# First-stage norms moved from DVE to ACT, and a new order of work at the stage's edges

## The chip, the cores and the metric

One core of a Trainium2 chip runs one program of 38,066 instructions. The engines are PE (TensorE), DVE (VectorE), ACT (ScalarE), POOL (GpSimd) and SP (SyncE, which here only issues DMAs); each takes its own instructions in order, and they meet at semaphores. The metric is the device time of one execution in microseconds (us).

## The reference, cut to what matters

16 batches of 112 tokens of width 256 pass through four blocks, each added to its input:

```python
x = x + tanh(g_xattn[0]) * L0_xattn(layernorm(x), ctx_1024, mask, ...)   # 16 heads of 16, 375 keys
x = x + tanh(g_ffn[0])   * L0_ffn(layernorm(x), Wg, We, be)              # 8 experts, the best 2 weighed
x = x + tanh(g_xattn[1]) * L1_xattn(ctx_1024, layernorm(x), ...)         # 16 heads of 64
x = x + tanh(g_ffn[1])   * L1_ffn(layernorm(x), W1, b1, W2, b2, Wr, br)  # routed experts
# layernorm(x) = (x - mean) / sqrt(var + 1e-5)
```

The first two lines are the kernel's first stage; the change lies in it. Both of its layer norms are of a [112, 256] tile, one row per token.

## The kernel before

The program has three stages, one after the other: `phase_attention_small_heads` (tiles named a_, the first 455 us), `phase_attention_large_heads` (b_) and `phase_experts` (c_). The first loops over 16 batches. Each engine has its own `body(b, par)`, and on PE, ACT and DVE a body has 16 slots, one per head. The order within an engine is written out by hand; there is no scheduler. In slot s of batch b:

- PE: scores of head s (L610), transposes of the probabilities of head s-2 (L618), values of head s-4 (L632), then items;
- DVE: `maxima` of head s (L853), `plo` of head s-2 (L858), the low half of the transposed probabilities;
- ACT: `exps` of head s-1 (L717), `phi` of head s-2 (L724), the high half of the same.

Numbers are carried as two f16 halves, high and low. `plo` of a head needs `phi` of that head, `phi` needs PE's transposes, and these need the exponential. The scores have two buffers, so PE can be at most two heads ahead of DVE.

In between, the slots hold the projections of the next batch (`item`, P_K keys, P_XT the transposed tokens, P_Q queries, P_V values: table PSLOT) and the expert block of the batch before (`ditem`: D_XT, D_GATE, D_PAIRS, D_CWT, D_BIAS: tables DSLOT and DREAD). On ACT the items of a slot stand ahead of its exponential.

The two norms. For the tokens of batch b+1: DVE's `stats_x` and `moments_x` in slot 0 (L813, L817), POOL's `deviation_x` (L431 variance plus eps, L433 the power -1/2), DVE's `norm_x` at the end of slot 1 (L823), then PE's transposes (L549). For x1, the output of the attention of batch b-1: POOL's `residual` makes x1 (L456, L459, L463), DVE's `stats_x1` in slot 5 (L874, L876), POOL's `deviation_x1` (the same lines), DVE's `norm_x1` at the end of slot 6 (L829), PE's transposes (L580), ACT's and DVE's halves (L701, L882), the gate and the four products of pairs of experts (L527, 128x512).

The weights of the second stage are read from HBM in eight loads of 512 KB (`load_next`, ACT's queue, L740, in the even batches from 2 on and once more in batch 14) and split in 16 parts: `next_high` on ACT (L746) in slots 8 to 15 of batch 14 and 0 to 7 of batch 15, `next_low` on POOL (L473) inside `sum_experts`. The buffer `next_f` first holds the expert weights of this stage (`we_f`, 2 MB), read at the start by ACT's queue and split in batch 0 (L734, L468).

Keys and queries pass through HBM to be stacked: SP writes them out (`keys_out` L342, `queries_out` L356) and reads them back in six DMAs each (`stack_keys` L350, `stack_queries` L364). SP's order for batch 0 is: load the tokens and context of batch 1 (L325, L327), keys out, key stacks, queries out, query stacks. ACT, before its items of batch 0, waits for the setup loads and takes the tanh of the gates (L793); DVE does `norm_x(0)` between the low halves of the weights, copies bq, waits for the tanh, and then does its items.

Of the kernel before, what the change touches and what calls it, by code (L numbers as in the profile page):

```python
# [64 lines left out]
def need(eng, sem, per, batch, count, met=None):  # L65

    need_all(eng, met, (sem, per, batch, count))
# [29 lines left out]
def ahead(b, n):  # L99

    return not (isinstance(b, int) and b + n > B - 1)

def phase_attention_small_heads(nc, x, ctxT, mask, g_xattn, g_ffn, wq, wk, wv, bq, bk, bv, wg, we, be, consts,
# [3 lines left out]
    with ExitStack() as ctx:  # L107
# [40 lines left out]
        rstd = sb("rstd", [T, 1], F32)  # L148
        xn = sb("xn", [T, D], F32)
# [32 lines left out]
        rstd1 = sb("rstd1", [T, 1], F32)  # L182
        xn1 = sb("xn1", [T, D], F32)
# [103 lines left out]
                 14: [D_PAIRS[3]], 15: [D_BIAS]}  # L287

# [14 lines left out]
        def _(sp):  # L303
# [93 lines left out]

            load_tokens(1)
            keys_out(0, 0)
            stack_keys(0, 0)  # L400
            queries_out(0, 0)
# [10 lines left out]
        def _(pool):  # L412
# [15 lines left out]
            def deviation(c, s_in, s_mid, s_out, stat, mid, out):  # L428

                need(pool, s_in, 2, c, 2, settled)  # L430
                pool.tensor_scalar(mid[:, :], stat[:, 1:2], 1.0, EPS, ALU.mult, ALU.add).then_inc(s_mid, 1)  # L431
                need(pool, s_mid, 1, c, 1)
                pool.tensor_tensor(out[:, :], mid[:, :], neg_half[0:T, :], ALU.pow).then_inc(s_out, 1)  # L433

            def deviation_x(c):
                deviation(c, s_stats, s_var, s_rstd, mv, var, rstd)

            def deviation_x1(c):
                deviation(c, s_stats1, s_var1, s_rstd1, mv1, var1, rstd1)
# [35 lines left out]
            def sum_experts(c, alone=True):  # L475

                for j in range(E // 2):
                    if not alone:
                        for n in range(2):
                            next_low((c - (B - 3)) * 8 + 2 * j + n)  # L480
                    need(pool, s_scaled, E // 2, c, j + 1)
                    need(pool, s_odd if j else s_x2, E // 2 if j else 1, c, j)
                    pool.tensor_tensor(acc_odd[:, :], scaled[j % 2][:, :], (acc_odd if j else x1)[:, :], ALU.add).then_inc(s_odd, 1)
                need(pool, s_odd, E // 2, c, E // 2)
                need(pool, s_dfree, DI, c, DI)
                need(pool, s_store, 16, c, 0)
                pool.tensor_tensor(x2[:, :], acc_odd[:, :], acc[:, :], ALU.add).then_inc(s_x2, 1)

            def body(b, par):
                if ahead(b, 1):  # L490
                    deviation_x(b + 1)
                if not first(b):
                    residual(b - 1)
                    deviation_x1(b - 1)
                if ahead(b, 1):
                    mask_bias(b + 1, 1 - par)
                    split_queries(b + 1)
                if ahead(b, 2):
                    split_context(b + 2)
                if not first(b):  # L500
                    sum_experts(b - 1, ahead(b, 2))
                if first(b):
                    for n in range(H // 2):
                        experts_low(n)
# [168 lines left out]
        def _(act):  # L673
# [40 lines left out]

            def exps(b, par, h):
                need(act, s_max, H, b, h + 1)
                act.activation(prob[:, h % RING, :], prob[:, h % RING, :], ACT.Exp, bias=top[:, h % RING:h % RING + 1],  # L717
                               scale=-1.0, accum_out=sums[par][:, h:h + 1]).then_inc(s_exp, 1)
# [17 lines left out]
            def load_next(col):  # L736


                act.wait_ge(s_welo, H // 2)
                act.dma_start(next_f[:, bass.ds(col, NLOAD)], next_w_dram[:, bass.ds(col, NLOAD)]).then_inc(s_nload, 16)  # L740

            def next_high(n):

                if n == 0:
                    act.wait_ge(s_nload, 16 * 8)
                act.activation(next_w[:, HI, n * NEXT:(n + 1) * NEXT], next_f[:, n * NEXT:(n + 1) * NEXT], ACT.Copy).then_inc(s_nhi, 1)  # L746
# [6 lines left out]
            def body(b, par):  # L753
                for s in range(H):
# [14 lines left out]
                    if par == 0 and not first(b) and s == 0:  # L769
                        load_next(b * (NLOAD // 2) - NLOAD)  # L770
                    if isinstance(b, int) and b == B - 2 and s == H // 4:
                        load_next(b * (NLOAD // 2))
                    if not ahead(b, 2) and (s >= H // 2) == ahead(b, 1):
                        next_high((s + H // 2) % H)
# [13 lines left out]
            for n, (lo, hi) in enumerate(WPARTS):  # L788
                act.wait_ge((s_wk, s_wq, s_wv)[n], 32 if n else 16)
                act.activation(wqkv[:, HI, :, lo:hi], wqkv_f[:, :, lo:hi], ACT.Copy).then_inc(s_whi, 1)  # L790
            act.wait_ge(s_const, 50)
            act.wait_ge(s_setup, NSETUP)
            act.activation(tanhs[:, :], gates[:, :], ACT.Tanh).then_inc(s_tanh, 1)  # L793
            act.dma_start(we_f[:, :, :], we).then_inc(s_wload, 16)
            for k in range(PI):
                item(0, 0, k)
# [4 lines left out]
            out_lo(B - 1)  # L801
            ditem(B - 1, D_XT)
# [5 lines left out]
        def _(dve):  # L808
# [9 lines left out]

            def norm_x(c):

                need(dve, s_rstd, 1, c, 1)
                need(dve, s_item, PI, c, 0)
                dve.tensor_scalar(xn[:, :], x_in[:, :], mv[:, 0:1], rstd[:, 0:1], ALU.subtract, ALU.mult).then_inc(s_xn, 1)  # L823

            def norm_x1(c):

                need(dve, s_rstd1, 1, c, 1)
                need(dve, s_ditem, DI, c, 0)
                dve.tensor_scalar(xn1[:, :], x1[:, :], mv1[:, 0:1], rstd1[:, 0:1], ALU.subtract, ALU.mult).then_inc(s_xn1, 1)  # L829
# [101 lines left out]
            def body(b, par):  # L931
                for s in range(H):
# [21 lines left out]
                    if ahead(b, 1) and s == 1:  # L954
                        norm_x(b + 1)
                    if not first(b):
                        if s == 9:
                            rank_experts(b - 1)
                        if s == 5:
                            stats_x1(b - 1)  # L960
                        if s == 6:
                            norm_x1(b - 1)

# [3 lines left out]
            for n, (lo, hi) in enumerate(WPARTS):  # L967
                dve.wait_ge(s_whi, n + 1)
                dve.tensor_tensor(wqkv[:, LO, :, lo:hi], wqkv_f[:, :, lo:hi], wqkv[:, HI, :, lo:hi], ALU.subtract).then_inc(s_wlo, 1)
                if n == 0:  # L970
                    stats_x(0)
                    moments_x(0)
                if n == 1:
                    norm_x(0)
            dve.wait_ge(s_const, 48)
            for e in range(2):
                rows = slice(64 * e, 64 * e + 64)
                dve.tensor_copy(bq_c[rows, :], bq_g[rows, e::2]).then_inc(s_const, 1)
# [3 lines left out]
            for k in range(PI):  # L982
                item(0, 0, k)
# [5 lines left out]
            norm_x1(B - 1)  # L989
# [1365 lines left out]
```

## Time and profile before

| | |
|---|---|
| median of 3 runs | 1407.45 us (1403.61 to 1407.69) |
| profiled execution | 1406.79 us, its span 1405.0 us |
| PE busy | 1225.0 us (87%) |
| DVE busy | 1083.2 us (77%) |
| ACT busy | 999.4 us (71%) |
| POOL busy | 813.3 us (58%) |

The span is what the trace covers; the profiled execution's time lies 1.8 us above it. Busy shares are means over three stages with different limits. In a timeline row the first number is the start in us, the second the duration; an instruction can start some 0.1 us before the one ahead of it on its engine ends. Ends of matmuls are modelled.

### The profile page before, as it was taken

Reading aid. Unit: us, or ns where it says so; the run is one execution under the profiler, and the core shown is the slowest. Engines: PE = TensorE matmul, PEld = TensorE weight load, DVE = VectorE, ACT = ScalarE, POOL = GpSimd, SP = SyncE. Lnnn points to the kernel's source line nnn. Section 1 sums busy time; section 2 is a strip of 40 time slices with the busy share of each in tenths; the row PEclk is TensorE's granted clock in tenths of the full one; section 3 lists DMA queues with packets and bytes.
Section 4 is the critical chain, followed back from the end, with each engine's and each line's share of the span. In section 5 each row is a group of like instructions: output and inputs, shape, how many; then the busy total and the mean of one; then the engine's idle time right before and its main releaser. Section 6 shows DMA issues by size and latency. Waiting matters only on the chain. (4 is left out here: it accounts for less than half of the span.)

```text
span 1405.0 us, 38066 instructions
## 1 busy us (share of the span) xinstructions
PE 1225.0 (87%) x13060; PEld 880.3 (63%) x13060; DVE 1083.2 (77%) x3112; ACT 999.4 (71%) x2552; POOL 813.3 (58%) x1204
## 2 busy tenths in 40 slices
PE   3999999999986499999999999999999974489994
PEld 1777777777764245566656566656666653389894
DVE  3799999999985168888888888888888882477872
ACT  2888888888883358877787887787888771256562
POOL 3544444444454346677777777777777674146564
PEclk7799999999987599999999999999999985699997
DMA  5444545455420148877788777878777793854333
GB/s 162 131 146 144 148 120 169 114 151 155 134 50 7 49 94 156 141 147 146 153 158 160 143 146 154 147 151 163 152 144 152 137 196 61 316 154 60 57 36 76
DMA packets 309406, 185.50 MB, mean 132 GB/s; under 512 B 257930, under 2 KB 295186, under 8 KB 306112
## 3 DMA queue, kind: packets, MB, share of 16 engines
q1 hardware_dynamic: 293024, 140.82, 47.3%
q0 software_dynamic: 13168, 35.80, 10.5%
q10 hardware_dynamic: 3024, 6.47, 1.5%
q8 instruction: 106, 1.74, 0.5%
q14 instruction: 84, 0.69, 0.2%
HBM read 76.19 MB, written 49.94 MB: 90 GB/s over the span
## 5 line engine op out<-in xcount | busy, mean ns | idle before, releaser
L1682 ACT ACTIVATE b_prob<-b_prob,b_top 112x487 f32<-112x487 f32 x256 | 178.9, 699 | 28.3 <-DVE b_top L1808 26.5
L1315 POOL TENSOR_TENSOR b_halves<-b_prob,b_halves 112x487 f16<-112x487 f32 x128 | 146.9, 1148 | 83.7 <-ACT b_halves L1707 82.2
L1493 PE MATMUL b_ps_p<-w_s,b_tok_s 128*128 128x512 f16 (+1 forms) x768 | 187.7, 381 | 4.0 <-DVE b_k_s L1795 3.2
L1493 PE MATMUL b_ps_p<-b_tok_s,w_s 128*128 128x487 f16 x768 | 181.9, 374 | 6.6 <-POOL b_tok_s L1309 3.7
L1808 DVE CUSTOM_DVE_ANT_0 b_prob<-b_ps_s,b_keep 112x487 f32<-112x487 f32 x256 | 167.3, 655 | 13.2 <-PE b_ps_s L1586 11.6
L717 ACT ACTIVATE a_prob<-a_prob,a_top 112x375 f32<-112x375 f32 x256 | 154.8, 605 | 3.7 <-DVE a_top L853 2.0
L1707 ACT ACTIVATE b_halves<-b_prob 112x487 f16<-112x487 f32 x256 | 156.0, 609 | 0.6
L853 DVE CUSTOM_DVE_ANT_0 a_prob<-a_ps_s,a_keep 112x375 f32<-112x375 f32 x256 | 138.1, 540 | 21.7 <-PE a_ps_s L610 21.4
L618 PE MATMUL a_ps_t<-a_const,a_prob 112*125 112x112 f32 x768 | 135.7, 287 | 10.6 <-ACT a_prob L717 9.1
L1601 PEld LDWEIGHTS b_ps_o<-b_v_s,b_pT 128*128 128x128 f16 (+1 forms) x3072 | 123.9, 99 | 31.4 <-DMA b_pT<-b_halves 11.6
L1601 PE MATMUL b_ps_o<-b_v_s,b_pT 128*128 128x64 f16 (+1 forms) x3072 | 135.0, 195 | 9.2 <-DMA b_pT<-b_halves 9.1
L858 DVE TENSOR_TENSOR a_pT<-a_ps_t,a_pT 125x336 f16<-125x336 f32 x256 | 128.1, 500 | 19.2 <-ACT a_pT L724 18.7
L618 PEld LDWEIGHTS a_ps_t<-a_const,a_prob 112*125 112x125 f32 x768 | 117.5, 196 | 36.1 <-ACT a_prob L717 28.1
L1493 PEld LDWEIGHTS b_ps_p<-b_tok_s,w_s 128*128 128x128 f16 x768 | 66.0, 98 | 95.1 <-issue 20.3
L1493 PEld LDWEIGHTS b_ps_p<-w_s,b_tok_s 128*128 128x128 f16 (+1 forms) x768 | 70.7, 105 | 83.5 <-DVE b_k_s L1795 12.5
L1795 DVE TENSOR_TENSOR b_k_s<-b_ps_p,b_k_s 128x487 f16<-128x487 f32 x128 | 84.5, 661 | 49.9 <-ACT b_k_s L1663 49.9
L1813 DVE TENSOR_TENSOR b_halves<-b_prob,b_halves 112x487 f16<-112x487 f32 x128 | 120.9, 945 | 0.0
L724 ACT ACTIVATE a_pT<-a_ps_t 125x336 f16<-125x336 f32 x256 | 113.5, 443 | 2.3 <-PE a_ps_t L618 2.2
L1670 ACT ACTIVATE b_v_s<-b_ps_p 128x512 f16<-128x512 f32 (+1 forms) x128 | 76.2, 595 | 53.1 <-PE b_ps_p L1493 52.1
L1803 DVE TENSOR_TENSOR b_v_s<-b_ps_p,b_v_s 128x512 f16<-128x512 f32 (+1 forms) x128 | 87.9, 686 | 31.7 <-ACT b_v_s L1670 31.7
L1586 PE MATMUL b_ps_s<-b_k_s,b_q_s 64*112 64x487 f16 x768 | 107.1, 385 | 0.3 <-DVE b_top L1808 0.3
L1663 ACT ACTIVATE b_k_s<-b_ps_p 128x487 f16<-128x487 f32 x128 | 72.8, 570 | 41.6 <-PE b_ps_p L1493 40.2
(263 smaller groups left out, 3022.9 us busy)
## 6 DMA issues: line engine op xcount, KB each, us to landing
xs<-a_blank SPq DMA_DIRECT2D x14, 1032.0 KB, 4.5
c_w_pool<-w_split SPq DMA_DIRECT2D x8, 1600.0 KB, 10.6
b_wch_f<-in_w_experts POOLq DMA_DIRECT2D x32, 384.0 KB, 5.2
w_split<-b_wch_s POOLq DMA_DIRECT2D x32, 384.0 KB, 3.9
a_k_stack<-keys SPq DMA_DIRECT2D x96, 93.8 KB, 3.1
a_ctx_f<-in_ctxT SPq DMA_DIRECT2D x16, 375.0 KB, 3.8
keys<-a_k_s SPq DMA_DIRECT2D x16, 375.0 KB, 3.2
b_ctx_t<-in_ctx SPq DMA_DIRECT2D x16, 375.0 KB
```

Source lines behind the costliest of these rows:

```text
L618: last = pe.transpose(ps_t[h % 2][0:KB0, j * T:(j + 1) * T], prob[:, h % RING, j * KB0:(j + 1) * KB0], ident[0:T, 0:T])
L717: act.activation(prob[:, h % RING, :], prob[:, h % RING, :], ACT.Exp, bias=top[:, h % RING:h % RING + 1], scale=-1.0, accum_out=sums[par][ ...
L724: act.activation(pT[0:KB0, h % RING, HI, :, 0:T], ps_t[h % 2][0:KB0, 0:NB0 * T].rearrange("p (j n) -> p j n", j=NB0), ACT.Copy).then_inc(s ...
L853: dve.tensor_tensor_reduce(prob[:, h % RING, :], ps_s[h % 2][0:T, 0:C], keep[par][:, :], -SCALE0, 3e38, ALU.add, ALU.min, top[:, h % RING: ...
L858: dve.tensor_tensor(pT[0:KB0, h % RING, LO, :, 0:T], ps_t[h % 2][0:KB0, 0:NB0 * T].rearrange("p (j n) -> p j n", j=NB0), pT[0:KB0, h % RIN ...
L1315: pool.tensor_tensor(halves[:, h % TURN, LO, 0:NK], prob[:, h % RING, 0:NK], halves[:, h % TURN, HI, 0:NK], ALU.subtract).then_inc(s_lo[1], 1)
L1493: last = pe.matmul(out, sta(a, k), mov(m, k), start=(k == 0 and n == 0), stop=(k == tiles - 1 and n == 2))
L1601: last = pe.matmul(ps_o[h // 8][:, col:col + D1], pT[0:k, h % TURN, a, j, :], v_s[par][0:k, m, j, h * D1:(h + 1) * D1], start=(h % 8 == 0 ...
L1682: act.activation(prob[:, h % RING, 0:NK], prob[:, h % RING, 0:NK], ACT.Exp, bias=top[:, h % RING:h % RING + 1], scale=-1.0, accum_out=sums ...
L1707: act.activation(halves[:, h % TURN, HI, 0:NK], prob[:, h % RING, 0:NK], ACT.Copy).then_inc(s_hi, 1)
L1808: dve.tensor_tensor_reduce(prob[:, h % RING, 0:NK], ps_s[h % 3][0:T, 0:NK], keep[par][:, :], -SCALE1, 3e38, ALU.add, ALU.min, top[:, h % R ...
L1813: dve.tensor_tensor(halves[:, h % TURN, LO, 0:NK], prob[:, h % RING, 0:NK], halves[:, h % TURN, HI, 0:NK], ALU.subtract).then_inc(s_lo[0], 1)
```

## The change

It adds two 112x1 tiles for each norm, `away` (minus the mean) and `shift` (minus the mean times the reciprocal deviation). POOL computes both, one operation ahead of the power and one behind it. ACT computes `rstd * x + shift` in place of DVE's `(x - mean) * rstd`: for the tokens in slot 1, for x1 in slot 6, each time ahead of the slot's exponential. The weights of the second stage are loaded one part per batch in batches 2 to 9 and split two parts per batch in batches 4 to 11, on ACT in slots 2 and 6, on POOL after `split_queries` and after `sum_experts`. At the start SP sends keys and queries out first and only then issues the stacks; ACT and DVE do the items of batch 0 ahead of the tanh and of what waits for the setup loads; the 2 MB load of the expert weights is issued in slot 1 of batch 0.

```diff
@@ sync @@
+            keys_out(0, 0)
             load_tokens(1)
-            keys_out(0, 0)
+            queries_out(0, 0)
             stack_keys(0, 0)
-            queries_out(0, 0)
             sp.wait_ge(s_zq, 2)
             stack_queries(0, 0)
@@ gpsimd @@
-            def deviation(c, s_in, s_mid, s_out, stat, mid, out):
+            def deviation(c, s_in, s_mid, s_out, stat, mid, out, off, shift):
                 need(pool, s_in, 2, c, 2, settled)
                 pool.tensor_scalar(mid[:, :], stat[:, 1:2], 1.0, EPS, ALU.mult, ALU.add).then_inc(s_mid, 1)
-                need(pool, s_mid, 1, c, 1)
+                pool.tensor_scalar(off[:, :], stat[:, 0:1], -1.0, None, ALU.mult).then_inc(s_mid, 1)
+                need(pool, s_mid, 2, c, 2)
                 pool.tensor_tensor(out[:, :], mid[:, :], neg_half[0:T, :], ALU.pow).then_inc(s_out, 1)
+                need(pool, s_out, 2, c, 1)
+                pool.tensor_tensor(shift[:, :], off[:, :], out[:, :], ALU.mult).then_inc(s_out, 1)
...
                     split_queries(b + 1)
+                if 0 <= b - NEXT_SPLIT < H // 2:
+                    next_low(2 * (b - NEXT_SPLIT))
                 if ahead(b, 2):
                     split_context(b + 2)
                 if not first(b):
-                    sum_experts(b - 1, ahead(b, 2))
+                    sum_experts(b - 1)
+                if 0 <= b - NEXT_SPLIT < H // 2:
+                    next_low(2 * (b - NEXT_SPLIT) + 1)
@@ scalar @@
+            def norm_x(c):
+                need(act, s_rstd, 2, c, 2)
+                need(act, s_item, PI, c, 0)
+                act.activation(xn[:, :], x_in[:, :], ACT.Identity, bias=shift[:, 0:1], scale=rstd[:, 0:1]).then_inc(s_xn, 1)
...
-                    if par == 0 and not first(b) and s == 0:
-                        load_next(b * (NLOAD // 2) - NLOAD)
-                    if isinstance(b, int) and b == B - 2 and s == H // 4:
-                        load_next(b * (NLOAD // 2))
-                    if not ahead(b, 2) and (s >= H // 2) == ahead(b, 1):
-                        next_high((s + H // 2) % H)
+                    if first(b) and s == 1:
+                        act.dma_start(we_f[:, :, :], we).then_inc(s_wload, 16)
+                    if s == 0 and 0 <= b - NEXT_LOAD < H // 2:
+                        load_next(b - NEXT_LOAD)
+                    if s in NEXT_SLOTS and 0 <= b - NEXT_SPLIT < H // 2:
+                        next_high(2 * (b - NEXT_SPLIT) + NEXT_SLOTS.index(s))
+                    if ahead(b, 1) and s == 1:
+                        norm_x(b + 1)
+                    if not first(b) and s == 6:
+                        norm_x1(b - 1)
                     if not (first(b) and s < 1):
                         exps(*heads(s, 1, b, par))
...
+            norm_x(0)
             act.wait_ge(s_const, 50)
+            for k in range(PI):
+                item(0, 0, k)
             act.wait_ge(s_setup, NSETUP)
             act.activation(tanhs[:, :], gates[:, :], ACT.Tanh).then_inc(s_tanh, 1)
-            act.dma_start(we_f[:, :, :], we).then_inc(s_wload, 16)
-            for k in range(PI):
-                item(0, 0, k)
@@ vector @@
-                    if ahead(b, 1) and s == 1:
-                        norm_x(b + 1)
-                        if s == 6:
-                            norm_x1(b - 1)
```

DVE's copies of bq move ahead, behind the first moments, and its items of batch 0 ahead of the tanh, in the same way as ACT's. `norm_x1` on ACT has the form of `norm_x`. NEXT_LOAD is 2, NEXT_SPLIT 4, NEXT_SLOTS (2, 6).

## Rows read from the trace of the kernel before

**Rows 1.** Busy time of each engine in stretches: us, then busy us (instructions), granted clock, DMA.

```profile
257.31:260.72 3.41, 2.81 (x30) 2.19 (x28) 3.41 (x11) 3.32 (x11) 1.47 (x3) 1.00 0.42 117
180.00:240.00 60.00, 55.79 (x594) 45.42 (x595) 56.94 (x200) 51.83 (x158) 25.75 (x41) 1.00 0.51 148
```

**Rows 2.** Timeline of DVE, L813 in batch 2 and in batch 14: start, duration, instruction.

```profile
83.50 0.42 DVE L813 BATCH_NORM_STATS2 a_bns<-a_x_in 112x6 f32<-112x256 f32 x1
...
379.98 0.42 DVE L813 BATCH_NORM_STATS2 a_bns<-a_x_in 112x6 f32<-112x256 f32 x1
```

**Rows 3.** Timelines of ACT, POOL and DVE, slots 0 to 1 of one batch.

```profile
257.17 0.60 ACT L717 ACTIVATE a_prob<-a_prob,a_top 112x375 f32<-112x375 f32 x1
257.76 0.44 ACT L724 ACTIVATE a_pT<-a_ps_t 125x336 f16<-125x336 f32 x1
...
257.45 0.19 POOL L431 TENSOR_SCALAR a_var<-a_mv 112x1 f32<-112x1 f32 x1 [0.94 <-DVE a_mv L817]
257.72 0.56 POOL L433 TENSOR_TENSOR a_rstd<-a_var,a_neg_half 112x1 f32<-112x1 f32 x1
...
257.19 0.17 DVE L817 BATCH_NORM_AGGREGATE a_mv<-a_bns 112x2 f32<-112x6 f32 x1
...
258.24 0.50 DVE L858 TENSOR_TENSOR a_pT<-a_ps_t,a_pT 125x336 f16<-125x336 f32 x1
258.65 0.41 DVE L823 TENSOR_SCALAR a_xn<-a_x_in,a_mv,a_rstd 112x256 f32<-112x256 f32 x1
```

**Rows 4.** The same three timelines, slot 6 of that batch.

```profile
264.22 0.60 ACT L717 ACTIVATE a_prob<-a_prob,a_top 112x375 f32<-112x375 f32 x1
...
265.23 0.55 POOL L433 TENSOR_TENSOR a_rstd<-a_var,a_neg_half 112x1 f32<-112x1 f32 x1
...
265.61 0.50 DVE L858 TENSOR_TENSOR a_pT<-a_ps_t,a_pT 125x336 f16<-125x336 f32 x1
266.03 0.50 DVE L829 TENSOR_SCALAR a_xn<-a_x,a_mv,a_rstd 112x256 f32<-112x256 f32 x1
```

**Rows 5.** Groups of instructions by line, 100 to 340 us.

```profile
L712 ACT ACTIVATE a_scaled<-a_ps_p,a_cw 112x256 f32<-112x256 f32 x40 | 19.0, 475 | 13.8 <-PE a_ps_p L527 13.8
```

**Rows 6.** Timeline of all engines, the start of the kernel.

```profile
11.41 0.33 ACTq L794 DMA_DIRECT2D a_next_f<-in_we  x1
...
13.61 0.35 SPq L342 DMA_DIRECT2D keys<-a_k_s  x1
...
20.67 2.68 SPq L350 DMA_DIRECT2D a_k_stack<-keys  x6
...
26.81 2.65 SPq L364 DMA_DIRECT2D a_q_stack<-queries  x6
...
30.82 0.56 PE L610 MATMUL a_ps_s<-a_k_stack,a_q_stack 96*112 96x375 f16 x1 [14.13 <-DMA a_q_stack<-queries]
...
36.96 0.34 SPq L342 DMA_DIRECT2D keys<-a_k_s  x1
...
40.37 3.75 SPq L350 DMA_DIRECT2D a_k_stack<-keys  x6
```

**Rows 7.** Timeline of ACT, POOL and DVE in batch 15.

```profile
415.89 0.67 ACT L746 ACTIVATE w_s<-a_next_f 128x512 f16<-128x512 f32 x1
...
416.56 2.26 POOL L473 TENSOR_TENSOR w_s<-a_next_f,w_s 128x512 f16<-128x512 f32 x2
416.63 2.35 DVE L829 TENSOR_SCALAR a_xn<-a_x,a_mv,a_rstd 112x256 f32<-112x256 f32 x1
```

**Rows 8.** Stretches around a fall of the clock, and expert products at either clock.

```profile
405.11:408.53 3.42, 2.12 (x22) 1.64 (x23) 2.37 (x9) 3.42 (x12) 3.34 (x4) 1.00 0.00 0
408.53:411.94 3.41, 3.26 (x24) 2.46 (x23) 2.42 (x8) 3.41 (x11) 0.73 (x2) 0.50 0.24 67
...
269.14 1.48 PE L527 MATMUL a_ps_p<-a_we_s,a_x1T 128*112 128x512 f16 x6
...
422.33 2.79 PE L527 MATMUL a_ps_p<-a_we_s,a_x1T 128*112 128x512 f16 x6
```

## What I predict, and why

> **What bounds the kernel now.** The change touches only the first stage, about the first third of the page's slices, so I read that stage and nothing else: first the starts of one repeated DVE instruction, then the timelines of DVE, ACT, POOL and PE over one batch, then the start, the end and the granted clock. The statistics of the next batch's tokens are taken once per batch, just after a batch begins. From batch 2 to batch 14 there are 13 of them, and first and last lie 296.48 us apart, 24.71 us per batch [rows 2]. Every batch repeats to a hundredth, so what happens in one happens in all. Inside a batch the busy shares differ by part. In the stretch of slots 1 to 3, DVE is busy 3.41 of 3.41 us, ACT 3.32, PE 2.81; over 60 us of whole batches ACT is busy 51.83 [rows 1], so it idles 3.4 us per batch. DVE is full there, and ACT almost: that idle time lies nearly all in slots 9 to 14, beside the expert products. The reader should not take ACT's mean of 71% over the span as room in slots 1 to 8.
>
> The four engines run in lock step. In slot s, PE does scores of head s, DVE its maximum, ACT the exponential of head s-1 and the high half of the probabilities of s-2, DVE their low half. In slot 1 ACT's high half ran from 257.76 to 258.20 and DVE's low half began at 258.24 [rows 3]: 0.04 us of slack. Whatever delays ACT there delays DVE.
>
> **Part 1: the tokens' normalisation moves to ACT, at the head of slot 1.** It removes from DVE one instruction of 0.41 us, of which 0.32 lies on the path (it began at 258.65, and the next instruction starts some 0.1 before one ends) [rows 3]. On ACT it stands behind the first key item and ahead of the exponential of head 0, which began at 257.17 [rows 3]. ACT takes its instructions in order, so both that exponential and the high half behind it wait until the shift is there. When is that? The moments end at 257.36; POOL begins the variance at 257.45 and the power at 257.72, done at 258.28 [rows 3]. The change puts the negated mean between them (one more of 0.19, as the variance takes) and the product after the power: I take 0.25 and 0.30 with the gaps, so the shift lands at about 258.8. ACT can start at 258.85, and a 112x256 activation with a scale column takes 0.475 [rows 5], some 0.35 before the next can follow. So the exponential begins at 259.2 instead of 257.17: +2.03. DVE's low half, bound to ACT by 0.04 us, moves as much; less 0.32 saved, DVE's path is 1.71 us later. Can that be given back in slots 2 to 5? DVE and ACT are both full there, so no. Bounds: +1.2 if the two POOL operations cost only 0.1 each and ACT's own time partly hides, +2.3 if they cost 0.5 each.
>
> **Part 2: the second normalisation moves to ACT in slot 6.** In the same way: ACT reached the exponential of head 5 at 264.22; the power ended only at 265.78; DVE took the product at 266.03, its low half of head 4 having begun at 265.61 [rows 4]. With the shift 0.5 later, ACT normalises at 266.35 and the exponential starts at 266.7, 2.5 us late. ACT then does 0.6 for it and 0.44 for the high half, so the low half begins at about 267.75 instead of 265.61: +2.15. DVE's saving is 0.42, and POOL's mask operation no longer meets it. By adding up the slots I get +1.84 for this part (ACT is a little behind DVE already). Bounds +1.2 and +2.4. Both parts: +3.55 us per batch, in batches 1 to 14: 14 x 3.55 = +49.7. Batch 0 has the first wait only, beside a slower PE: +0.5.
>
> **Part 3: what the two holes do to the clock.** PE waits for the same exponentials: it will be idle about 1.4 us in slot 2 and 2.1 us in slot 7, on top of the small gaps it has. The trace of before has this once. At the batches' end, in slots 0 to 3 of batch 15, PE was busy 2.12 of 3.42 us, after which the clock stood at 0.50, that is 1.2 in place of 2.4 GHz, from 408.5 until dense expert products had run [rows 8]. Around the second hole PE will be less busy than that, so I expect the clock to fall in many batches and to rise again in the expert products. The price is in rows at either level: one such product took 1.48 us at full and 2.79 at half clock [rows 8], 1.3 more. If two of a batch's four run at half and slots 7 and 8 lose 0.5, that is +3.1 per batch, 14 x 3.1 = +43.4. Bounds: 0 (the clock stays) and 4 x 1.3 + 1.1 = 6.3 per batch, +88. I take the middle, since both ends have a row behind them and neither is nearer.
>
> **Part 4: the weights of the next stage.** Before, ACT rounded them 16 times in batches 14 and 15 (0.67 each, some 0.5 without the overlap) and POOL took the rest (2.26 for two) [rows 7]. Now two of each fall into batches 4 to 11. The one in slot 6 lies inside ACT's new wait and is free. The one in slot 2 stands where ACT is full: 8 x 0.5 = +4. POOL's second, at the end of a batch, may hold up the variance by 0.2 of a us, but where the clock is low the first is partly hidden. I take +4; bounds 0 and +6.5. The loads (512 KB each, one per batch) are waited for a batch or more later: nothing, unless the queues fill.
>
> **Part 5: the start.** Before, SP issued keys out at 13.61, and the stacking of keys only at 20.67, 7.1 us later, while ACT's load of 2 MB (issued 11.41) moved. Queries went out after all of the key stacking; their stacking began at 26.81 and the first scores at 30.82 [rows 6]. For the next keys, without that load, it is 36.96 to 40.37, 3.4 us [rows 6]. Now: the shift is ready at 10.5, ACT's key items follow at 10.9 without the wait for gates and tanh, keys go out at 12.8, the key stacks at 16.2; the queries go out at 15.7 in between, their stacks follow the key stacks at 19.1 and land by 23.1. First scores at 23.1 instead of 30.8: -7.7. If the key write takes 7 us also without the big load, little is left: -1. The big load is now issued in batch 0, slot 1, ten us before its first reader and with the key stacks of batch 1 beside it: +0.5, bounds 0 and +4. With batch 0's wait the start is -6.7.
>
> **Part 6: the end of the stage.** In batch 15 the eight roundings made ACT the bound of slots 0 to 7. The DVE product at 416.63 took 2.35 us while POOL's two ran 2.26 [rows 7]: it waited for POOL, and PE with it. Both go, some -4.5 if all counted. But the wait of part 2 comes here as well (+2) and PE at half clock needs about as long as ACT did. The tail has POOL's two extra operations bare, +0.5. I take -1.5, bounds -5 and +2.
>
> For that stall, the Trainium skill ("SBUF — State Buffer", section "Who interferes with whom") says that DVE in some modes and GpSimd share a port pair, and whoever starts first holds it for the whole instruction. The row agrees in kind; but DVE waited for both POOL instructions and not for one, 2.35 us where one would be 1.13. By the page the cure would be worth 1.1 us here, by the row 2.3. It also says that ACT never waits for it, which speaks for the change in batch 15 and nowhere else.
>
> **The sum.** The profiled execution took 1406.8 (span 1405.0), beside a median of 1407.5. 1406.8 - 6.7 + 49.7 + 43.4 + 4 - 1.5 = 1495.7, so 1496.
>
> **The rivals.** A: the waits come, the clock stays up. For it: 13 batches ran at full clock with small gaps. Against: the fall of [rows 8] with a busier PE. 1495.7 - 43.4 = 1452. B: the clock is at half for most of each batch and PE binds throughout, 10 us per batch instead of 3.1: about 1590. Against: expert products raised the clock before. C, on the other side: the normalisations cost nothing on ACT, because it comes to them later than I think, and DVE, which is full [rows 1], gains 0.32 + 0.42 per batch: 1406.8 - 14 x 0.74 - 6.7 - 1.5 = 1388. It decides if ACT reaches the normalisation 1.7 us later against the moments than it does now. Speaks for it: ACT idles 3.4 us per batch. Against: where that lies, and DVE's moments come after the high half that ACT gives it, so ACT is always ahead. D: the change doesn't bring its start (the key write is slow by itself): +6.7 on any of these; it is in the range.
>
> **Chances.** The forecast 0.60 (its own range 1465 to 1540), A 0.25 (1440 to 1465), B 0.08, C 0.07. The range 1440 to 1540 holds the first two. Faster by over 0.3% (about what a measurement can tell from no change) 0.06, within 0.3% 0.02, slower 0.92.
>
> **What would show it.** Parts 1 and 2: on ACT, two idle gaps per batch ended by POOL's shift, 1.6 and 2 us, ahead of the two normalisations; the DVE low half behind them waits for ACT as long; the batch 28 us apart at full clock, 31 to 32 with half-clock stretches. Part 3: the granted clock's mean over 100 to 380 us, 1.00 before, well below it. Part 5: first scores near 23 us. The prediction is wrong if DVE shows no such idle time, or if the batch is 24 us.

## Result and profile after

The changed kernel takes 1470.2 us (median of 4, 1468.6 to 1471.0) beside 1405.5 us (median of 4, 1403.1 to 1407.7): ratio 1.0457, 95% interval 1.0436 to 1.0478, 64.7 us slower. The profiled execution took 1471.0, its span 1469.2 (1405.0 before, 64.2 less than now). I had forecast 1496, with a range of 1440 to 1540. Three runs that took far longer than the others of their kernel (5930.5 and 3288.0 us of before, 1631.9 us in one experiment) stand in no median here.

All of it is in the first stage. Its last addition on POOL (the output of the last batch) began at 454.27 before and begins at 519.06 now, 64.8 later. First the stretch from 60 to 380 us: us, then busy us (instructions) of PE, PEld, DVE, ACT and POOL, granted clock, DMA share, GB/s. Of after:

```profile
60.00:380.00 320.00, 272.44 (x2539) 221.22 (x2537) 245.63 (x860) 239.81 (x714) 144.35 (x239) 0.89 0.42 121
```

and of before:

```profile
60.00:380.00 320.00, 298.89 (x3108) 241.46 (x3106) 302.59 (x1074) 271.61 (x828) 142.37 (x218) 1.00 0.49 141
```

DVE, which was nearly full (302.6 of 320), is now idle for 74 us, and the clock's mean is 0.89. What DVE and the others wait for, 110 to 385 us, after (us in total, times, longest):

```profile
DVE a_pT L874 <- ACT a_pT L747: 53.2, 53, 2.4
...
PE a_ps_t L629 <- ACT a_prob L740: 36.6, 27, 2.3
ACT a_xn L730 <- POOL a_shift L443: 16.5, 9, 1.9
...
ACT a_xn L736 <- POOL a_shift L443: 8.5, 9, 2.1
```

This is the chain of parts 1 and 2: POOL's shift, ACT, DVE and PE. The batches, by the same instruction as [rows 2], in batches 2 and 14 of after:

```profile
80.21 0.42 DVE L841 BATCH_NORM_STATS2 a_bns<-a_x_in 112x6 f32<-112x256 f32 x1
...
443.22 0.42 DVE L841 BATCH_NORM_STATS2 a_bns<-a_x_in 112x6 f32<-112x256 f32 x1
```

That is 363.0 us for 12 batches, 30.25 each, beside 24.71: +66.5. Batch 1 has +2.8, the time up to the statistics of batch 0 -6.1, batch 0 nothing, and from the last statistics to the stage's end it is 75.84 beside 74.29: +1.6. These five make the 64.8.

Slots 0 to 2 of batch 7, timelines of POOL, ACT, DVE and PE (to be held against [rows 3]):

```profile
232.53 1.16 POOL L483 TENSOR_TENSOR w_s<-a_next_f,w_s 128x512 f16<-128x512 f32 x1
233.78 0.19 POOL L438 TENSOR_SCALAR a_var<-a_mv 112x1 f32<-112x1 f32 x1
234.04 0.24 POOL L439 TENSOR_SCALAR a_away<-a_mv 112x1 f32<-112x1 f32 x1
234.37 0.56 POOL L441 TENSOR_TENSOR a_rstd<-a_var,a_neg_half 112x1 f32<-112x1 f32 x1
235.00 0.19 POOL L443 TENSOR_TENSOR a_shift<-a_away,a_rstd 112x1 f32<-112x1 f32 x1
...
235.23 0.60 ACT L730 ACTIVATE a_xn<-a_x_in,a_shift,a_rstd 112x256 f32<-112x256 f32 x1 [1.89 <-POOL a_shift L443]
235.73 0.59 ACT L740 ACTIVATE a_prob<-a_prob,a_top 112x375 f32<-112x375 f32 x1
...
236.78 0.51 DVE L874 TENSOR_TENSOR a_pT<-a_ps_t,a_pT 125x336 f16<-125x336 f32 x1 [2.39 <-ACT a_pT L747]
...
236.47 0.58 PE L629 MATMUL a_ps_t<-a_const,a_prob 112*125 112x112 f32 x3 [1.99 <-ACT a_prob L740]
```

ACT idles 1.89 us for the shift, and behind it DVE idles 2.39 and PE 1.99. POOL's half of a rounded weight (232.53) stands ahead of the variance and holds it until 233.78; the moments were there at 233.43. The second hole, in slot 6 ([rows 4] before):

```profile
244.54 0.62 ACT L769 ACTIVATE w_s<-a_next_f 128x512 f16<-128x512 f32 x1
245.66 0.60 ACT L736 ACTIVATE a_xn<-a_x,a_shift,a_rstd 112x256 f32<-112x256 f32 x1 [0.49 <-POOL a_shift L443]
...
247.22 0.51 DVE L874 TENSOR_TENSOR a_pT<-a_ps_t,a_pT 125x336 f16<-125x336 f32 x1 [1.74 <-ACT a_pT L747]
```

The clock in the same batch, in stretches of 2.2 us ([rows 8] before):

```profile
234.71:236.91 2.20, 0.44 (x4) 0.44 (x5) 0.13 (x1) 1.68 (x5) 1.13 (x3) 1.00 0.34 117
236.91:239.11 2.20, 1.42 (x14) 1.12 (x12) 1.78 (x5) 2.20 (x7) 0.00 (x0) 0.75 0.00 0
239.11:241.31 2.20, 2.20 (x23) 2.09 (x21) 2.20 (x10) 2.20 (x8) 0.00 (x0) 0.50 0.96 256
...
243.51:245.71 2.20, 2.20 (x20) 2.20 (x19) 1.48 (x6) 0.97 (x4) 1.17 (x5) 0.70 0.45 114
245.71:247.91 2.20, 1.35 (x16) 1.05 (x15) 0.69 (x2) 2.20 (x7) 2.05 (x4) 1.00 0.32 72
```

PE stands still for the first hole, its clock falls to 1.2 GHz behind it, it works through slots 3 to 6 at that clock, and is back at 2.4 GHz before the second hole. Around that one (the last row) PE was busy 1.35 of 2.20 us, and the clock stayed; ahead of the fall in [rows 8] it had been busy 2.12 of 3.42. Whole batches: batch 3, and batch 7.

```profile
111.26:142.68 31.42, 27.27 (x242) 22.17 (x241) 23.20 (x82) 22.20 (x66) 11.99 (x22) 0.84 0.40 121
...
232.51:262.54 30.03, 25.85 (x242) 21.24 (x241) 23.23 (x84) 22.90 (x68) 14.20 (x24) 0.89 0.41 125
```

The start ([rows 6] before), all engines:

```profile
11.60 1.01 ACT L701 ACTIVATE a_k_s<-a_ps_p,a_bk_c 128x375 f16<-128x375 f32 x2
...
13.40 0.34 SPq L349 DMA_DIRECT2D keys<-a_k_s  x1
...
17.19 2.79 SPq L357 DMA_DIRECT2D a_k_stack<-keys  x6
...
20.07 2.71 SPq L371 DMA_DIRECT2D a_q_stack<-queries  x6
...
24.71 0.56 PE L621 MATMUL a_ps_s<-a_k_stack,a_q_stack 96*112 96x375 f16 x1 [5.82 <-DMA a_q_stack<-queries]
```

From keys out to the key stacks it is 3.8 us where it was 7.1.

### The profile page after: what moved, and what is told of

Same layout as the page of the kernel before. It is cut to its first block and busy times, and to the rows that moved or that the text cites. A ratio compares the mean times of both kernels' runs of the same rounds, so it can differ in the third digit from the quotient of the medians.

```text
span 1469.2 us, 38137 instructions
## 1 busy us (share of the span) xinstructions
PE 1258.4 (86%) x13060; PEld 908.5 (62%) x13060; DVE 1071.0 (73%) x3080; ACT 1014.5 (69%) x2584; POOL 828.3 (56%) x1268
## 5 line engine op out<-in xcount | busy, mean ns | idle before, releaser
L629 PE MATMUL a_ps_t<-a_const,a_prob 112*125 112x112 f32 x768 | 150.0, 309 | 65.4 <-ACT a_prob L740 63.4
L1690 ACT ACTIVATE b_prob<-b_prob,b_top 112x487 f32<-112x487 f32 x256 | 178.8, 698 | 27.3 <-DVE b_top L1816 25.7
L629 PEld LDWEIGHTS a_ps_t<-a_const,a_prob 112*125 112x125 f32 x768 | 128.2, 214 | 100.7 <-ACT a_prob L740 93.5
L1609 PEld LDWEIGHTS b_ps_o<-b_v_s,b_pT 128*128 128x128 f16 (+1 forms) x3072 | 124.0, 99 | 31.2 <-DMA b_pT<-b_halves 11.9
L538 PE MATMUL a_ps_p<-a_we_s,a_x1T 128*112 128x512 f16 x384 | 102.6, 408 | 1.0
```

Source lines behind the costliest of these rows:

```text
L629: last = pe.transpose(ps_t[h % 2][0:KB0, j * T:(j + 1) * T], prob[:, h % RING, j * KB0:(j + 1) * KB0], ident[0:T, 0:T])
L1609: last = pe.matmul(ps_o[h // 8][:, col:col + D1], pT[0:k, h % TURN, a, j, :], v_s[par][0:k, m, j, h * D1:(h + 1) * D1], start=(h % 8 == 0 ...
L1690: act.activation(prob[:, h % RING, 0:NK], prob[:, h % RING, 0:NK], ACT.Exp, bias=top[:, h % RING:h % RING + 1], scale=-1.0, accum_out=sums ...
```

## Experiments

Three questions: are the waits at the two normalisations the cause, what does the clock add, and what do the rest of the change's parts bring? "Before" was run beside each group; its medians were 1405.5 (the start alone, both back on DVE, six idle products, normalisations later), 1405.4 (each alone, two more POOL operations), 1403.2 (ten idle products and the two with roundings in slots 11 and 14) and 1405.6 (the last). A batch is counted from one statistics instruction to the next, as above.

**The start alone.** Before with only the new order of part 5:

```diff
+            keys_out(0, 0)
             load_tokens(1)
-            keys_out(0, 0)
+            queries_out(0, 0)
             stack_keys(0, 0)
-            queries_out(0, 0)
...
+                    if first(b) and s == 1:
+                        act.dma_start(we_f[:, :, :], we).then_inc(s_wload, 16)
```

and ACT's and DVE's items of batch 0 ahead of the tanh.

> The kernel before with the new order at the start alone (keys and queries out first, items ahead of the tanh, the 2 MB load in batch 0); the norms on DVE, loads and splits of the next weights as before. The first scores moved from 30.8 to 24.7 us, so -6 us if nothing gives it back: 1399 to 1401 us. If the 2 MB load in batch 0 delays the expert weights and batch 1 (rival), less than 3 us is left: 1403 or above.

1399.2 us, ratio 0.9950 (0.9925 to 0.9975). The first scores come at 23.29, every batch from 2 to 13 takes 24.71, and the stage ends 7.9 us earlier than before:

```profile
12.89 0.34 SPq L342 DMA_DIRECT2D keys<-a_k_s  x1
...
19.03 2.72 SPq L364 DMA_DIRECT2D a_q_stack<-queries  x6
...
23.29 0.56 PE L610 MATMUL a_ps_s<-a_k_stack,a_q_stack 96*112 96x375 f16 x1 [7.33 <-DMA a_q_stack<-queries]
```

In after they come at 24.71. Of these 1.4 us, 1.1 comes from the normalisation of batch 0 on ACT, ahead of the key items: with it on DVE and the rest of the change in place (the next kernel) they come at 23.57. The other 0.3 was not followed.

**Both normalisations back on DVE.** After, with `norm_x` and `norm_x1` on DVE as before and POOL's negated mean and product gone; the start and the spread roundings stay.

> The changed kernel with both norms back on DVE and POOL's two added operations gone; start, loads and splits of the next stage's weights as changed. Theory 1 and 2 both expect a batch of 24.7 to 25.2 us and 1395 to 1403 us: everything lost lies in the norms, the start's 6 us is kept. If instead the spread splits cost (theory 3: ACT full in slot 2 of batches 4 to 11), 8 of the batches are 0.5 us longer or more and the time is 1404 or above.

1397.9 us, ratio 0.9939 (0.9916 to 0.9962): 72 us below after. So the two normalisations, with POOL's operations for them, are the whole loss. Batches without roundings are back at 24.71; those with them take 25.38, or 26.3 and 26.4 in two where the clock fell.

**Each alone.** After with only the tokens' normalisation on ACT, and with only that of x1:

> The changed kernel with only the tokens' norm (slot 1) on ACT, x1's back on DVE. Theory 1 prices the wait of slot 1 at 2.0 to 2.5 us per batch less 0.32, and the clock falls behind the hole as before: a batch of 27 to 28.5 us, 1430 to 1450 us. If the wait of slot 1 were absorbed, 1400.

> The changed kernel with only x1's norm (slot 6) on ACT, the tokens' back on DVE. Alone, this wait is not shortened by a slow PE ahead of it, so theory 1 prices it at about 2 us per batch less 0.42 and a part of a clock fall: a batch of 26.3 to 28 us, 1420 to 1445 us. If e5 and e6 together lose more than the changed kernel does, the two waits overlap through the clock; if less, they add to something of their own.

1440.3 (1.0242, 1.0225 to 1.0259) and 1447.3 us (three runs, 1441.5 to 1449.0; 1.0283, 1.0251 to 1.0315), the second somewhat above what I expected. Over 1397.9 they cost 42.4 and 49.3, together 91.7, where both at once cost 72.3. Two delays of one path would add up; these overlap. At full clock they do add: with only x1's on ACT, batch 2 (no roundings, clock 1.00) takes 26.85, 2.14 over 24.71, and this wait is worth 2.11 below, where both are there. What overlaps is the clock's part. With only x1's on ACT the batches come in two kinds, here batches 7 and 8:

```profile
220.29:251.10 30.81, 27.44 (x242) 21.99 (x241) 23.59 (x85) 22.73 (x67) 13.82 (x22) 0.83 0.41 123
251.10:278.34 27.24, 23.38 (x242) 18.64 (x241) 23.30 (x85) 22.34 (x67) 13.80 (x22) 1.00 0.46 138
```

The same instructions take 27.24 us when the clock stays and 30.81 when it falls: 3.6 us for one fall. It fell here behind the hole of slot 7, and stayed at half through slots 8 to 10 and the first expert products:

```profile
235.69:237.89 2.20, 2.20 (x24) 1.95 (x21) 1.75 (x7) 1.51 (x5) 1.34 (x1) 0.50 0.57 158
237.89:240.09 2.20, 2.20 (x7) 1.15 (x6) 1.05 (x6) 0.83 (x4) 0.00 (x0) 0.50 0.08 18
```

PE is busy without a pause, DVE for 1.75 and 1.05 us of the 2.20 and ACT for 1.51 and 0.83: PE sets the pace. That is the term of part 3 much as I had priced it (3.1).

**Two more POOL operations.** After, with two more dependent 112x1 products in each chain, whose result nobody reads:

```diff
...
+                for i in range(2):
+                    need(pool, s_mid, 4, c, 2 + i)
+                    pool.tensor_scalar(spare[:, :], stat[:, 0:1], -1.0, None, ALU.mult).then_inc(s_mid, 1)
...
```

> The changed kernel with two more dependent 112x1 operations on POOL ahead of each power, some 0.55 us more until each shift. If both norms' waits lie bare on the path (theory 1), each batch is 0.8 to 1.1 us longer, 11 to 16 us in all: 1481 to 1487 us. If it is ACT's own work or the clock that sets the batch (theory 2), 0 to 4 us.

1487.1 us, ratio 1.0574 (1.0557 to 1.0592). From the negated mean to the power it is 0.90 us here and 0.33 in after, 0.57 more. Where the clock goes as it does in after, twice 0.57 comes out: batches 5, 7 and 10 take 31.2 us beside 30.0, 1.2 more, so POOL's chain lies bare on the path. The whole, 16.9, is some 30 times 0.57 with 32 normalisations in the stage, but that it fits so well is luck. Batches 2, 3 and 13 are 0.7 to 0.9 shorter than in after, since there no fall came behind the second hole, and batches 6 and 9 are 3.4 and 3.2 longer (33.43 and 33.19), since there one did.

**Idle products in the holes.** After, with PE given six, then ten, products of 512 columns in slots 2 and 7 of batches 1 to 14, ahead of the transposes that wait; their results are never read.

```diff
+                        if s in FILL and ahead(b, 1) and not first(b):
+                            need(pe, s_max, H, b, s)
+                            for i in range(FILL[s]):
+                                pe.matmul(ps_s[(s + 1) % 2][:, 0:512], wqkv[:, HI, 0, 0:128], wqkv[:, HI, 1, 0:512], start=True, stop=True)
```

> The changed kernel with six idle 512-column matmuls on PE (1.3 us at full clock) in each of the two holes of batches 1 to 14, into a score bank that is free there; their results are read by nobody. If the half clock behind the holes costs 1 to 3 us a batch, the clock now stays up more and the time falls by 10 to 30 us, to 1440 to 1460. If the clock's falls cost nothing (the waits alone fill the 5.5 us a batch), the time is the same or up to 8 us more.

> The kernel after with ten idle 512-column products (their result is never read) in place of six on PE ahead of the transposes in slots 2 and 7 of batches 1 to 14: some 2.1 us of work at full clock, as long as the holes. Theory 1 (the waits alone set the batch, and the clock's fall hides in the second wait): a granted clock nearer to 1.00 than the 0.93 that six gave, and a time that does not fall below about 1460; where a batch runs wholly at full clock it still takes 28.5 us or more. Theory 2 (the clock costs 3 us a batch, as the forecast had it): batches at full clock of 28.2 us or less, and 1440 or below if the clock stays up. A loss of up to 10 us over the six (1467.3) would say that the fillers themselves stand in the path at half clock, and would leave the question to the single batches.

1467.4 (1.0430, 1.0403 to 1.0457) and 1459.7 us (1.0410, 1.0392 to 1.0429). The first gains 2.8 us where I had expected 10 to 30 or nothing; the second came out as theory 1 has it. Six kept the clock up in three of batches 2 to 13, ten in ten of these twelve. Batches 3 and 6 with ten, and for comparison batch 3 with six:

```profile
108.24:137.00 28.76, 27.67 (x262) 20.55 (x261) 22.99 (x84) 21.74 (x66) 11.99 (x22) 1.00 0.43 131
195.77:225.25 29.48, 27.70 (x262) 20.37 (x261) 23.06 (x82) 22.77 (x68) 14.17 (x24) 1.00 0.43 128
```

```profile
107.71:136.47 28.76, 26.29 (x254) 19.61 (x253) 22.99 (x84) 21.74 (x66) 11.99 (x22) 1.00 0.43 131
```

With six or with ten it is 28.76, so four more fillers in each hole cost nothing there; that the first six don't either is concluded from it. This is then the changed kernel at 2.4 GHz throughout: 28.76 - 24.71 = 4.05 us for the two waits, and 29.48 - 28.76 = 0.7 for the roundings: ACT's in slot 2 is bare (0.5), and ACT waits 1.88 for the first shift where it waits 1.64 without them, since POOL's half stands ahead of the variance. After's own batches 4 to 11 take 29.8 to 30.0 instead of 29.5, its batches 2 and 3 31.05 and 31.42 instead of 28.7. Here is the split of the 4.05, by DVE in batch 3 with ten:

```profile
109.52 0.61 DVE L862 SCALAR_TENSOR_TENSOR a_k_s<-a_ps_p,a_bk_c,a_k_s 128x375 f16<-128x375 f32 x1
112.27 0.51 DVE L879 TENSOR_TENSOR a_pT<-a_ps_t,a_pT 125x336 f16<-125x336 f32 x1 [2.14 <-ACT a_pT L752]
...
121.68 0.51 DVE L879 TENSOR_TENSOR a_pT<-a_ps_t,a_pT 125x336 f16<-125x336 f32 x1 [2.27 <-ACT a_pT L752]
```

Against the batch's statistics, the first of these low halves begins 4.03 us in and was at 1.80 before: +2.23, less 0.31 for the instruction that left DVE. At the second the offset grows by another 2.35, less 0.42, and 0.18 is lost at the transposes behind it. 1.92 + 2.11 is 4.03 of the 4.05.

**The same normalisations, later.** After, with `norm_x` in slot 2 behind the exponential, and `norm_x1` in slot 7 behind the high half; so the shift is there when ACT comes. Then the same with ACT's roundings in slots 11 and 14 instead of 2 and 6, POOL's halves one batch later.

```diff
-                    if ahead(b, 1) and s == 1:
-                        norm_x(b + 1)
-                    if not first(b) and s == 6:
-                        norm_x1(b - 1)
...
                         exps(*heads(s, 1, b, par))
+                    if ahead(b, 1) and s == 2:
+                        norm_x(b + 1)
...
                         phi(c, h)
+                    if not first(b) and s == 7:
+                        norm_x1(b - 1)
```

> The changed kernel with the two norms left on ACT, but the tokens' norm behind the exponential of slot 2 and x1's behind the high half of slot 7. If the wait for POOL's shift at the place of the norms is what costs (theory 1), ACT reaches both norms after the shift is there, no engine waits for them, PE has no holes and the clock stays at 1.00: a batch of 24.5 to 25.5 us and 1390 to 1405 us in all. If it is the work that ACT takes over in slots where it is full (theory 2), the place changes little: a batch stays above 27.5 us and the time above 1430 us.

> The kernel after with both normalisations on ACT, but late (as in the run with late normalisations, 1423.7 us), and ACT's two roundings of the next stage's weights per batch moved from slots 2 and 6 to slots 11 and 14 of batches 4 to 11 (POOL's halves of them one batch later). Theory 1 (what was left of the price with late normalisations is that ACT is full in slots 1 to 8: 0.60 + 0.60 us of normalisation a batch, and the roundings on top): the batches without roundings stay at about 26.8 to 27.4 us, those with them fall from some 27.4 to about 26.8; 1423.7 less 8 x 0.6 gives about 1416 to 1420. Theory 2 (the roundings were the cause, and the normalisations are free when they come late): batches of 25 us or less in 4 to 11, 1405 or below. Theory 3 (the remaining price is the half-clock stretches after the holes, and the roundings fed them): a granted clock of 1.00 between 60 and 380 us, and about 1405 to 1412.

1423.7 (1.0125, 1.0099 to 1.0150) and 1423.1 us (1.0179, 1.0111 to 1.0247; one of its four runs took 1438.8). The first lies between what the two theories gave, a miss for both: the waits were most of the loss (46.5 of the 72.3 go with them), but a normalisation on ACT is not free either. The second missed as well: moving the roundings brought nothing, and the granted clock did not stay up. At full clock a batch with roundings takes 26.75 in the first and 26.76 in the second, one without 25.76 in both: in either place they cost 1.0. A batch without roundings at full clock, of the second kernel, and DVE's waits in it:

```profile
104.60:130.36 25.76, 23.02 (x242) 18.69 (x241) 22.98 (x82) 21.89 (x66) 11.97 (x22) 1.00 0.49 146
...
108.46 0.51 DVE L874 TENSOR_TENSOR a_pT<-a_ps_t,a_pT 125x336 f16<-125x336 f32 x1 [0.58 <-ACT a_pT L747]
109.97 0.51 DVE L874 TENSOR_TENSOR a_pT<-a_ps_t,a_pT 125x336 f16<-125x336 f32 x1 [0.24 <-ACT a_pT L747]
...
116.85 0.39 DVE L898 TENSOR_TENSOR a_x1T<-a_ps_p,a_x1T 128x224 f16<-128x224 f32 x1 [0.68 <-ACT a_x1T L712]
```

25.76 is 1.05 more than with the normalisations on DVE: ACT, full in slots 1 to 8, carries 0.6 us more twice, and DVE waits 1.50 for it to save 0.73. Each of the three waits costs some 0.1 on top, because an instruction that had to wait doesn't start ahead of the other's end. Batches with a fall of the clock take 26.8 without ACT's roundings and 27.3 to 28.7 with them.

**Roundings, placed.** The kernel with both normalisations on DVE (1397.9), first with the roundings in ACT's slots 11 and 14, then in slots 9 (behind the high half) and 11, with one of POOL's two between the operations of the residual.

> The kernel after with both normalisations back on DVE (1397.9 us), and in addition the two roundings per batch moved from ACT's slots 2 and 6 to slots 11 and 14, where ACT idles, with POOL's halves one batch later. Theory 1 (the roundings cost 0.5 to 0.7 us a batch because ACT is full where they stand): batches 4 to 11 fall from 25.38 to 24.7 or 24.8 us, about 1392 to 1395. Theory 2 (their price is not their place but POOL's work on the shared memory side or the loads of 512 KB): batches stay at 25.3, 1397 to 1399.

> Both normalisations on DVE, the new start, and the roundings of the next stage's weights placed by what the run with slots 11 and 14 showed: there the one in slot 11 moved nothing, the one in slot 14 moved DVE's low half behind it by 0.52 us, and POOL's even half ahead of the context's low half made DVE's rank conversion wait 0.33 us. Here ACT's two stand at the end of slot 9 (ahead of ACT's 1.5 us wait for the gate) and in slot 11, and POOL's even half stands between its two residual operations, where it idles. Theory 1 (each cost was one of place): batches 4 to 11 take 24.7 to 24.85 us instead of 25.48, 1388 to 1390.5 in all against 1394.8. Theory 2 (a rounding costs its time wherever it stands): 25.4 us and 1394 or more. The mishap that would spoil it: POOL's moved half meets a DVE instruction without PSUM operand in slot 3, up to 1.1 us a batch, 1398 or more.

The first, 1394.8 us (0.9939, 0.9922 to 0.9957), has the time of its theory 1, but not the batches: 5 to 11 still take 25.48, so the place in slots 2 and 6 was not the only bad one. Its DVE and POOL show where the 0.77 goes. In batch 6:

```profile
188.74 1.61 POOL L433 TENSOR_TENSOR a_ctx_s<-a_ctx_f,a_ctx_s 128x750 f16<-128x750 f32 x1
...
189.87 0.50 DVE L928 CAST a_place_f<-a_place 112x8 f32<-112x8 uint32 x1
...
199.09 0.51 DVE L875 TENSOR_TENSOR a_pT<-a_ps_t,a_pT 125x336 f16<-125x336 f32 x1 [0.84 <-ACT a_pT L742]
```

The wait of 0.84 is 0.32 in a batch without roundings: the rounding in slot 14 stands right ahead of the work that DVE needs. And the conversion of 8 columns takes 0.50 us instead of 0.17: it ended at 190.37, when POOL's subtraction, pushed 1.1 us later by its half of a rounding, ended (190.35). It takes 0.50 or 0.51 in batches 5 to 12, where POOL has halves, and 0.17 in all others. The two costs can be had apart: batch 4 has ACT's roundings alone and takes 25.23 (+0.52), batch 12 has POOL's halves alone and takes 24.96 (+0.25); together they are the 0.77. The Trainium skill ("SBUF — State Buffer", section "Who interferes with whom") says that GpSimd and a DVE instruction in a two-port mode, which a cast can enter, share a pair of ports, and that whoever issues first holds it for its whole instruction. This row agrees to 0.02 us.

The second kernel, 1391.2 us, ratio 0.9899 (0.9882 to 0.9916), 0.7 above the range of its theory 1, has both gone. Batch 6, with two roundings on ACT and two on POOL in it:

```profile
174.63:199.33 24.70, 23.06 (x242) 18.65 (x241) 23.42 (x84) 21.94 (x66) 13.30 (x20) 1.00 0.53 153
```

It is the fastest of all: the start brings 7.9 us of the stage, the sixteen roundings taken out of batches 14 and 15 another 6.9 (its stage ends at 439.48, the start alone at 446.37), and no batch pays for them.

## Why the prediction was right, and where it was not

The sign and the waits were right, the price of the clock was not, and the time was 26 us too high. That it still lies in the forecast's own range (from 1465) and not in that of rival A (up to 1465) hangs on 5 us, and is in part luck. I go by the prediction's parts; its terms for the same stretches were -7.2 (start), +0.5 (batch 0), +6.65 (batch 1), +83.8 (batches 2 to 13), +5.15 (14 and 15); measured were -6.1, 0, +2.8, +66.5 and +1.6.

- **Parts 1 and 2, the waits: right, a little low.** 3.55 per batch forecast, 4.05 measured at full clock (1.92 for 1.71, 2.12 for 1.84). The shift came about when I had it (ACT's normalisation 1.55 us after the moments' end, 1.49 forecast); the miss is in ACT's own time. I took 0.475 and 0.35 to the next instruction from an activation with another source and without a bias column [rows 5]; it took 0.60 and 0.50. In 12 batches: 48.6 beside 42.6. The 1.84 of part 2 is more than the working shown there gives (2.15 less 0.42 is 1.73). In batch 1, which begins at half clock in both kernels, ACT waited only 0.43 for the first shift, 1.2 less than in batch 2; 4.05 less 1.2 is about the 2.8 that it takes more.
- **Part 3, the clock: the term that was wrong.** 3.1 per batch forecast, 37.2 in 12 batches. In batches 2 to 13 after takes 363.0 us, the kernel with ten fillers 352.5, of which some 1.5 are its own two batches with a fall: about 12 us for 12 batches, 1.0 each. The fall itself and its price were right: 3.6 for one behind the second hole with the expert products at half clock. What failed is the step that put it "around the second hole". In batches 4 to 11 the clock fell behind the first hole and rose before the second. There ACT came 1.6 us later to slot 6 (12.65 us into batch 7, 11.06 into batch 6 with ten fillers), but the shift only 0.54 later (13.15 and 12.61), so that ACT waited 0.49 where at full clock it waits 1.55:

```profile
208.38 0.60 ACT L741 ACTIVATE a_xn<-a_x,a_shift,a_rstd 112x256 f32<-112x256 f32 x1 [1.55 <-POOL a_shift L444]
```

The slow stretch ate the wait behind it, and my sum had paid both. In batches 2, 3 and 13, where a fall behind the second hole did reach the expert products, it cost 2.3 to 2.7. Why it came in these and not in others stays open. That they have no roundings is not the reason: with two more POOL operations it came in batches 6 and 9, which have them, and in none of 2, 3, 12 and 13.

- **Part 4: right, a little low.** +4 forecast; 0.7 in each of eight batches, about 6: the 0.5 of slot 2, and 0.24 at the variance, which I had named and not added. But "ACT is full there" is not the whole of it: with the normalisations on DVE the roundings cost as much in slots 11 and 14, and there POOL's halves shift POOL's other work onto DVE's cast (0.43 to 0.51 instead of 0.17), which I had left out. In after the cast takes 0.17 in every batch.
- **Part 5: right.** -7.7 to the first scores forecast, -7.5 with the start alone. In after -6.1: the normalisation of batch 0 on ACT takes 1.1 back, ahead of the key items. I had counted it, but too early: the shift at 10.5 and the key items at 10.9, where ACT normalised at 11.09 and went on at 11.60, and the queries went out at 16.82 and not at 15.7.
- **Part 6: two errors, the same way.** With the normalisations on DVE, from the last statistics to the stage's end it takes 67.5 instead of 74.3: -6.8, more than the 4.5 that I allowed. In after, +1.6: waits and clock in batches 14 and 15 and the tail take 8.4 where I had about 10.
- **The rivals.** A (clock up, 1452) is refuted as it stood, since the clock did fall; but its time was nearer than mine, 18 us off and not 26, mostly because the falls cost 1.0 a batch and not 3.1. C (ACT comes late enough, nothing is lost) was built with the late normalisations: not even then is it free, since ACT has no room in slots 1 to 8.

Not shown: how the loss of clock is shared out within a batch of after, beyond the difference to a batch at full clock: 0.5 us with roundings, 2.3 to 2.7 without, in three batches of four.

## What to carry to other kernels

Before an operation is moved to another engine, ask not how busy that engine is but when it reaches the place: an engine that takes its work in order and runs ahead of its neighbours has no room for an input that comes later than it does. Two costs that follow one another on one path (a hole, and a slower clock after it) are not added until it is clear that the second does not eat the next hole. Idle products that keep all else equal, and rows of single batches instead of the mean, separated them here.

## What was not expected of the hardware

- A 112x256 activation with scale and bias columns, f32 from and to SBUF, took 0.60 us on ACT, 0.51 to the start of the next; from PSUM with a scale column it was 0.475 [rows 5].
- One 112x1 operation more on POOL costs 0.26 to 0.33 us from start to start, of which 0.19 to 0.24 is its own.
- The clock answered to holes of PE that differ little: with x1's normalisation alone on ACT it fell in one batch (30.81) and stayed in the next (27.24), with the same instructions in both.
- A DVE cast of 8 columns took 0.50 us instead of 0.17 while a POOL subtraction of 1.61 us ran, and ended 0.02 us after it.
